# Final residual stage of a two-layer sandwich block: pairs of tiles against single tiles in a two-buffer ring

## The chip, the cores and the metric

The kernel runs on the eight NeuronCores of one Trainium2 chip. Each core computes 2,048 of the 16,384 tokens; the cores exchange nothing. The metric is the device time of the slowest core in microseconds.

## The reference

All of it is in float32; the kernel computes the matmuls in bf16.

```python
# x: [4, 4096, 4096]; W_attn, W_base: [4096, 4096]; 8 experts of rank 16, top 2
x = x + layernorm(layernorm(x) @ W_attn.T + b_attn)
y = layernorm(x)
w = top-2 softmax weights of y @ W_router.T, renormalised
lora = einsum('ter,eor,te->to', einsum('td,erd->ter', y, lora_A), lora_B, w) * 2.0
x = x + layernorm(y @ W_base.T + b_base + lora)
```

## The kernel before, in words

Everything is stored transposed: the feature index lies on the 128 partitions, the tokens along the free dimension. A core takes its tokens in four chunks (`ch`) of `C` = 512, and within a chunk the 4,096 features are 32 tiles (`k`) of 128 x 512. `xt` holds the chunk's x in float32 (32 tiles), `u` the normalised input of a matmul in bf16, `zb` the output of a matmul in bf16.

The instructions of the five engines are written out in order by hand, with semaphores: `s_t`, `s_v`, `s_s`, `s_gc` count finished instructions of TensorE, VectorE (DVE), ScalarE (ACT) and GpSimd (POOL); `s_x` counts x loads (one for each group of 8 tiles), `s_w` weight loads, and `s_o[0]`, `s_o[1]` output stores from the buffers `ost0` and `ost1`. Each engine works through its list in order, and a wait holds whatever stands behind it on that engine.

A chunk runs through these stages:

1. x load and statistics (L217 to L252). ScalarE issues the load of a group of 8 tiles (L227), after waiting at L221 until POOL has done the final add of the eighth tile of that group in the previous chunk (`f6k[8 * g + 7]`), since that add still reads `xt`. Then it makes a bf16 copy (L233) and a square (L234) of each of the 8 tiles, and TensorE sums both over the features. The load of the next group stands behind these on ScalarE.
2. The row statistics (`ln_rows`, `bc_pair`), and DVE's normalised `u` (L269 to L276).
3. 32 weight tiles of 128 x 4224 and their matmuls into `P` (L344), evacuated by ScalarE into `zb` (L328). POOL's queue issues the weight loads (L290, L301); in the first chunk the weights come in float32 and SP's queue stores them back in bf16 (`wsc`) for the other chunks.
4. Statistics, and the first residual add into `xt` (L370 to L379), in pairs of tiles.
5. Statistics of the new x, `u` again (L426 to L433), the router, and the low-rank part.
6. The second matmul with 32 weight tiles (L538), evacuated in the same way.
7. Statistics, and the final residual stage (L559 to L583): for each tile, DVE subtracts the mean from `zb` into `yb[k % 2]` and multiplies by the inverse deviation in place, POOL adds `xt` and writes `ost[k % 2]` in float32 (L574), and SP's queue stores it to `out` (L578), 256 KB.

Stage 7 is the one that the diff touches. DVE takes its tiles in pairs: two subtractions (L565, L567), one wait for the second of them, two multiplies (L570, L571), and before every pair but the first the waits of L562 to L564 for the stores of both buffers and for the add of the previous odd tile. POOL adds the two tiles one after the other, and each store is issued after its own add. On POOL's list the next chunk's first two weight loads stand behind the last add of stage 7. ScalarE's stage 1 of the next chunk runs beside stage 7 of this one, as far as the wait of L221 lets it.

Of the kernel before, what the change touches and what calls it, by code (L numbers as in the profile page):

```python
# [14 lines left out]
C = 512  # L15
NCH = TOK // C
KT = D // 128
# [6 lines left out]
def build_nc():  # L24
# [10 lines left out]
    outd = nc.dram_tensor("out", [D, TOK], F32, kind="ExternalOutput").ap()  # L35
# [3 lines left out]
    cnt = {"t": 0, "v": 0, "s": 0, "g": 0, "gc": 0,  # L39
           "x": [0, 0, 0, 0], "w": [0, 0], "o": [0, 0], "wsc": [0, 0]}  # L40

    def emit(e, fn):
        ops[e].append(fn)

    def wait(e, sem, val):
        if val > 0:
            emit(e, lambda eng, sem=sem, val=val: eng.wait_ge(sem, val))

    with ExitStack() as _es:
        xt = _es.enter_context(nc.sbuf_tensor("xt", [128, KT * C], F32))  # L50
        u = _es.enter_context(nc.sbuf_tensor("u", [128, KT * C], BF16))
        zb = _es.enter_context(nc.sbuf_tensor("zb", [128, OC * C], BF16))
# [16 lines left out]
        mbc_bf = _es.enter_context(nc.sbuf_tensor("mbc_bf", [128, C], BF16))  # L69
        ibc_bf = _es.enter_context(nc.sbuf_tensor("ibc_bf", [128, C], BF16))  # L70
# [36 lines left out]
        s_v = _es.enter_context(nc.semaphore("s_v"))  # L107
# [12 lines left out]
        s_gc = _es.enter_context(nc.semaphore("s_gc"))  # L120
# [4 lines left out]
        ost = [ost0, ost1]  # L125
# [3 lines left out]
        s_o = [s_o0, s_o1]  # L129
# [10 lines left out]
        def v_inc(fn):  # L140
            cnt["v"] += 1
            emit("V", lambda v, fn=fn: fn(v).then_inc(s_v, 1))
            return cnt["v"]

        def s_inc(fn):
            cnt["s"] += 1
            emit("S", lambda s, fn=fn: fn(s).then_inc(s_s, 1))
            return cnt["s"]

        def g_inc(fn):  # L150
            cnt["gc"] += 1
            emit("G", lambda g, fn=fn: fn(g).then_inc(s_gc, 1))
            return cnt["gc"]
# [25 lines left out]
        nout = 0  # L179
# [33 lines left out]
        f6k = {}  # L213
        for ch in range(NCH):
            t_pair = {}
            s_pair = {}
            for k in range(KT):  # L217
                if k % 8 == 0:
                    g = k // 8
# [45 lines left out]
            yb = [ybf0, ybf1]  # L265
            for kp in range(0, KT, 2):
                if kp >= 2:
# [3 lines left out]
                r2 = v_inc(lambda v, kp=kp: v.tensor_sub(  # L271
                    yb[1][:], xt[:, (kp + 1) * C:(kp + 2) * C], mbc_bf[:]))
# [94 lines left out]
            for kp in range(0, KT, 2):  # L367
                if kp >= 2:
# [3 lines left out]
                r2 = v_inc(lambda v, kp=kp: v.tensor_sub(  # L372
                    yb[1][:], zb[:, (kp + 1) * C:(kp + 2) * C], mbc_bf[:]))
                wait("V", s_v, r2)
                vc0 = v_inc(lambda v: v.tensor_mul(yb[0][:], yb[0][:], ibc_bf[:]))  # L375
                vc1 = v_inc(lambda v: v.tensor_mul(yb[1][:], yb[1][:], ibc_bf[:]))
# [30 lines left out]
            r = v_inc(lambda v: v.tensor_scalar_mul(row_a[:], ps_sqq[0:1, :], 1.0 / D))  # L407
            wait("V", s_v, r)
            r = v_inc(lambda v: v.tensor_mul(row_b[:], row_m[:], row_m[:]))
            wait("V", s_v, r)  # L410
            r = v_inc(lambda v: v.tensor_sub(row_a[:], row_a[:], row_b[:]))
# [4 lines left out]
            r = s_inc(lambda s: s.activation(row_b[:], row_a[:], AF.Ln))  # L416
# [6 lines left out]
            for kp in range(0, KT, 2):  # L423
                if kp >= 2:
# [3 lines left out]
                r2 = v_inc(lambda v, kp=kp: v.tensor_sub(  # L428
                    yb[1][:], xt[:, (kp + 1) * C:(kp + 2) * C], mbc_bf[:]))
# [29 lines left out]
            for tt in range(4):  # L459
# [17 lines left out]
                r2 = v_inc(lambda v, tt=tt: v.reduce_max(m2s[:, tt:tt + 1], l2t[:],  # L477
                                                         axis=AX.X))
# [78 lines left out]
            vv_stats_read = va  # L557
            bc_f = bc_pair(row_zm, va, sa, vv_apply_bank_free, s_free_need=vv_u_done)
            wait("V", s_s, bc_f)  # L559
            for kp in range(0, KT, 2):  # L560
                if kp >= 2:
                    wait("V", s_o[0], cnt["o"][0])  # L562
                    wait("V", s_o[1], cnt["o"][1])
                    wait("V", s_gc, f6k[kp - 1])  # L564
                v_inc(lambda v, kp=kp: v.tensor_sub(yb[0][:],  # L565
                                                    zb[:, kp * C:(kp + 1) * C], mbc_bf[:]))
                r2 = v_inc(lambda v, kp=kp: v.tensor_sub(  # L567
                    yb[1][:], zb[:, (kp + 1) * C:(kp + 2) * C], mbc_bf[:]))
                wait("V", s_v, r2)
                vc0 = v_inc(lambda v: v.tensor_mul(yb[0][:], yb[0][:], ibc_bf[:]))  # L570
                vc1 = v_inc(lambda v: v.tensor_mul(yb[1][:], yb[1][:], ibc_bf[:]))  # L571
                for k, vc in ((kp, vc0), (kp + 1, vc1)):
                    wait("G", s_v, vc)
                    f6k[k] = g_inc(lambda g, k=k: g.tensor_add(  # L574
                        ost[k % 2][:], yb[k % 2][:], xt[:, k * C:(k + 1) * C]))
                    wait("Y", s_gc, f6k[k])
                    def ostore(y, ch=ch, k=k):
                        return y.dma_start(  # L578
                            outd[k * 128:(k + 1) * 128, ch * C:(ch + 1) * C],
                            ost[k % 2][:]).then_inc(s_o[k % 2], 16)  # L580
                    emit("Y", ostore)
                    nout += 1
                    cnt["o"][k % 2] += 16  # L583
            vv_f6_done = cnt["v"]
            sv_zb_free = cnt["v"]
            vv_apply_bank_free = cnt["v"]
# [84 lines left out]
```

## Time and profile before

| | us |
|---|---|
| median of the runs | 3528.05 (3523.74 to 3532.36, 2 runs) |
| time of the profiled execution | 3537.88 |
| its span, slowest core (core 1) | 3536.3 |
| its spans, all cores | 3508.0 to 3536.3 |

| engine or transfer | busy us or share | count |
|---|---|---|
| TensorE matmul | 2381.8 (67%) | 10204 |
| DVE | 531.3 (15%) | 1243 |
| ScalarE | 544.5 (15%) | 1001 |
| POOL | 434.2 (12%) | 521 |
| x loads, `xt<-xT` | 10.3 us from issue to landing, 2048 KB each | 16 |
| output stores, `out<-ost` | 2.1 us from issue to landing, 256 KB each | 128 |

Busy shares are averages over stages with different limits, so they don't say what bounds a stage. The chain that ended last is followed back from the last instruction, at each step to what released it; "issue" in it is time in which the engine waited for nothing that the profile shows, and where an instruction begins before its forerunner has ended, only the part up to that start is counted. DVE is VectorE, POOL is GpSimd, ACT is ScalarE, ACTq and SPq are the queues that issue transfers. Times are microseconds from the span's start.

### The profile page before, as it was taken

To read this page: it belongs to the slowest core of one execution; us is meant where nothing else is said; L and a number is where in the kernel's file an instruction comes from. 1 tells how busy PE (TensorE), PEld (TensorE's weight loads), DVE (VectorE), ACT (ScalarE), POOL (GpSimd) and SP (SyncE) were. 2 spreads that over 40 slices of the span, in tenths; PEclk is the share of its full clock that TensorE was granted. 3 is DMA by queue.
4 is the path that set the end of the run, shared out by engine and by line. 5 is a ranking of instruction groups with operands and counts; after the bars stand their busy time and mean duration, and the time that the engine had idled before them with its cause. 6 is when DMAs were issued, how large, how long until landed. Compare 5 with 4: busy or idle time off the path is not lost.

```text
span 3536.3 us, 27097 instructions; the slowest of 8 cores (3508.0 to 3536.3 us)
## 1 busy us (share of the span) xinstructions
PE 2381.8 (67%) x10204; PEld 970.3 (27%) x10204; DVE 531.3 (15%) x1243; ACT 544.5 (15%) x1001; POOL 434.2 (12%) x521
## 2 busy tenths in 40 slices
PE   2677744787713998289922899359952699539980
PEld 0233311333200443034400344024420244114430
DVE  0400025000024000510012300340011400250002
ACT  3001021010121111211113011201102111211110
POOL 0000031000030001300021000400013000310003
PEclk7689965998855999589965799579975799659995
DMA  6399912888641442023333243013334143003422
GB/s 169 79 201 204 201 51 49 196 200 196 145 147 66 135 143 90 25 86 135 136 112 114 86 147 136 25 37 135 135 111 165 49 147 137 35 25 136 143 95 89
DMA packets 81887, 417.09 MB, mean 118 GB/s; under 512 B 7648, under 2 KB 7776, under 8 KB 40544
## 3 DMA queue, kind: packets, MB, share of 16 engines
q0 software_dynamic: 37472, 279.04, 29.6%
q1 hardware_dynamic: 27648, 102.77, 7.4%
q10 hardware_dynamic: 16640, 33.56, 2.9%
q8 instruction: 83, 1.36, 0.2%
q14 instruction: 44, 0.36, 0.0%
HBM read 383.98 MB, written 102.76 MB: 138 GB/s over the span
## 4 chain that ended last, share of the span: by engine, by line
PE 48%; DMA 22%; DVE 14%; issue 7%; POOL 5%; ACT 3%; DVEq 0%; POOLq 0%; ACTq 0%; SPq 0%
PE P L538 21%; PE P L344 20%; DMA wb<-wA 5%; DMA wb<-wF 5%; DMA out<-ost 4%; DMA wsc<-wb 4%; DMA xt<-xT 3%; POOL xt L379 3%; POOL ost L574 3%; PE ps_sq L310 1%; DVE ybf L269 1%; DVE ybf L426 1%; DMA wb<-wsc 1%; DVE ybf L428 1%; DVE ybf L271 1%
## 5 line engine op out<-in xcount | busy, mean ns | idle before, releaser
L344 PE MATMUL P<-u,wb 128*128 128x512 bf16 x4096 | 970.4, 395 | 161.2 <-DVE u L274 90.2
L538 PE MATMUL P<-u,wb 128*128 128x512 bf16 x4096 | 936.9, 388 | 77.4 <-DMA wb<-wF 66.8
L344 PEld LDWEIGHTS P<-u,wb 128*128 128x128 bf16 x4096 | 404.1, 100 | 720.8 <-issue 285.5
L538 PEld LDWEIGHTS P<-u,wb 128*128 128x128 bf16 x4096 | 403.9, 100 | 597.0 <-issue 147.2
L328 ACT CAST zb<-P 128x512 bf16<-128x512 f32 x256 | 150.0, 586 | 2030.1 <-PE P L349 835.1
L184 DVE TENSOR_SCALAR row_zm<-ps_sq 1x512 f32<-1x512 f32 x8 | 5.4, 679 | 2174.9 <-PE ps_sqq L316 2174.9
L242 PE MATMUL ps_sq<-xbf,ones 128*1 128x512 bf16 x128 | 56.8, 540 | 390.3 <-ACT sq L234 390.3
L301 POOL DMA_DIRECT2D wb<-wsc x192 | 101.5, 529 | 1701.6 <-PE P L546 846.5
L574 POOL TENSOR_TENSOR ost<-ybf,xt 128x512 f32<-128x512 bf16 x128 | 148.4, 1178 | 381.7 <-DVE ybf L570 367.2
L379 POOL TENSOR_TENSOR xt<-xt,ybf 128x512 f32<-128x512 f32 x128 | 147.8, 1173 | 212.7 <-DVE ybf L375 207.3
L396 PE MATMUL ps_sqq<-sq,ones 128*1 128x512 bf16 x64 | 37.4, 585 | 195.7 <-ACT sq L389 195.7
L329 ACT ACTIVATE sq<-P 128x512 bf16<-128x512 f32 x256 | 154.2, 602 | 0.0
L242 PEld LDWEIGHTS ps_sq<-xbf,ones 128*1 128x1 bf16 x128 | 7.3, 80 | 439.7 <-issue 439.7
L233 ACT CAST xbf<-xt 128x512 bf16<-128x512 f32 x128 | 77.5, 606 | 319.7 <-DMA xt<-xT 319.3
L443 PE MATMUL ps_mix<-rTs,u 128*128 128x8 bf16 x512 | 31.5, 167 | 130.5 <-DVE u L431 119.6
L389 ACT ACTIVATE sq<-xt 128x512 bf16<-128x512 f32 x128 | 80.6, 630 | 170.3 <-POOL xt L379 170.3
L234 ACT ACTIVATE sq<-xt 128x512 bf16<-128x512 f32 x128 | 79.9, 624 | 0.0
L565 DVE TENSOR_TENSOR ybf<-zb,mbc_bf 128x512 bf16<-128x512 bf16 x64 | 27.2, 425 | 328.0 <-DMA out<-ost 301.4
L396 PEld LDWEIGHTS ps_sqq<-sq,ones 128*1 128x1 bf16 x64 | 5.1, 79 | 255.7 <-issue 255.7
L310 PE MATMUL ps_sq<-zb,ones 128*1 128x512 bf16 x256 | 65.5, 378 | 11.0 <-ACT sq L329 11.0
L290 POOL DMA_DIRECT2D wb<-wA x32 | 16.9, 531 | 427.1 <-PE P L349 311.8
L443 PEld LDWEIGHTS ps_mix<-rTs,u 128*128 128x128 bf16 x512 | 23.7, 104 | 144.3 <-issue 144.3
(96 smaller groups left out, 1186.9 us busy)
## 6 DMA issues: line engine op xcount, KB each, us to landing
wb<-wsc POOLq DMA_DIRECT2D x192, 1056.0 KB, 5.9
wsc<-wb SPq DMA_DIRECT2D x64, 1056.0 KB, 8.4
wb<-wA POOLq DMA_DIRECT2D x32, 1056.0 KB, 11.7
wb<-wF POOLq DMA_DIRECT2D x32, 1056.0 KB, 11.2
xt<-xT ACTq DMA_DIRECT2D x16, 2048.0 KB, 10.3
out<-ost SPq DMA_DIRECT2D x128, 256.0 KB, 2.1
aTs<-aT POOLq DMA_DIRECT2D x1, 1024.0 KB, 14.2
bTs<-bT POOLq DMA_DIRECT2D x1, 1024.0 KB, 20.7
```

Of the source, the lines that this page charges most:

```text
L233: s_inc(lambda s, k=k: s.copy(xbf[k % 4][:], xt[:, k * C:(k + 1) * C]))
L234: s_pair[k] = s_inc(lambda s, k=k: s.activation(sq[k % 4][:], xt[:, k * C:(k + 1) * C], AF.Square))
L242: t_run(lambda t, j=j: t.matmul(ps_sq[0:1, :], ones128[:, 0:1], xbf[j % 4][:], start=(j == 0), stop=(j == KT - 1)))
L301: emit("G", lambda g, mat=mat, oc=oc, par=par: g.dma_start(wb[par][:], wsc[mat, oc]).then_inc(s_w[par], 16))
L310: t_run(lambda t, j=j: t.matmul(ps_sq[0:1, :], ones128[:, 0:1], zb[:, j * C:(j + 1) * C], start=(j == 0), stop=(j == OC - 1)))
L328: s_inc(lambda s, po=po: s.copy(zb[:, po * C:(po + 1) * C], P[po % 2][:]))
L329: ev[po] = s_inc(lambda s, po=po: s.activation(sq[po % 4][:], P[po % 2][:], AF.Square))
L344: t_run(lambda t, oc=oc, k=k: t.matmul(P[oc % 2][:], wb[oc % 2][:, k * 128:(k + 1) * 128], u[:, k * C:(k + 1) * C], start=(k == 0), stop=F ...
L379: c3k[k] = g_inc(lambda g, k=k: g.tensor_add(xt[:, k * C:(k + 1) * C], xt[:, k * C:(k + 1) * C], yb[k % 2][:]))
L389: s_pair[k] = s_inc(lambda s, k=k: s.activation(sq[k % 4][:], xt[:, k * C:(k + 1) * C], AF.Square))
L538: t_run(lambda t, oc=oc, k=k: t.matmul(P[oc % 2][:], wb[oc % 2][:, k * 128:(k + 1) * 128], u[:, k * C:(k + 1) * C], start=(k == 0), stop=F ...
L574: f6k[k] = g_inc(lambda g, k=k: g.tensor_add(ost[k % 2][:], yb[k % 2][:], xt[:, k * C:(k + 1) * C]))
```

## The change

Stage 7 no longer goes in pairs. Every tile has its own subtraction, its own wait and its own multiply, in the buffer `k % 2`. Before tile `k`, DVE waits for the store that last used the buffer `k % 2` (tile `k - 2`) and for the add of tile `k - 2`. Number, kind, shape and buffers of the instructions, POOL's adds and SP's stores stay as they are; the next chunk's wait on `f6k[8 * g + 7]` too. Stage 4, which has the same form of pairs, is not changed.

```diff
--- before.py
+++ after.py
@@ -557,30 +557,25 @@
             vv_stats_read = va
             bc_f = bc_pair(row_zm, va, sa, vv_apply_bank_free, s_free_need=vv_u_done)
             wait("V", s_s, bc_f)
-            for kp in range(0, KT, 2):
-                if kp >= 2:
-                    wait("V", s_o[0], cnt["o"][0])
-                    wait("V", s_o[1], cnt["o"][1])
-                    wait("V", s_gc, f6k[kp - 1])
-                v_inc(lambda v, kp=kp: v.tensor_sub(yb[0][:],
-                                                    zb[:, kp * C:(kp + 1) * C], mbc_bf[:]))
-                r2 = v_inc(lambda v, kp=kp: v.tensor_sub(
-                    yb[1][:], zb[:, (kp + 1) * C:(kp + 2) * C], mbc_bf[:]))
-                wait("V", s_v, r2)
-                vc0 = v_inc(lambda v: v.tensor_mul(yb[0][:], yb[0][:], ibc_bf[:]))
-                vc1 = v_inc(lambda v: v.tensor_mul(yb[1][:], yb[1][:], ibc_bf[:]))
-                for k, vc in ((kp, vc0), (kp + 1, vc1)):
-                    wait("G", s_v, vc)
-                    f6k[k] = g_inc(lambda g, k=k: g.tensor_add(
-                        ost[k % 2][:], yb[k % 2][:], xt[:, k * C:(k + 1) * C]))
-                    wait("Y", s_gc, f6k[k])
-                    def ostore(y, ch=ch, k=k):
-                        return y.dma_start(
-                            outd[k * 128:(k + 1) * 128, ch * C:(ch + 1) * C],
-                            ost[k % 2][:]).then_inc(s_o[k % 2], 16)
-                    emit("Y", ostore)
-                    nout += 1
-                    cnt["o"][k % 2] += 16
+            for k in range(KT):
+                if k >= 2:
+                    wait("V", s_o[k % 2], cnt["o"][k % 2])
+                    wait("V", s_gc, f6k[k - 2])
+                r = v_inc(lambda v, k=k: v.tensor_sub(yb[k % 2][:],
+                                                      zb[:, k * C:(k + 1) * C], mbc_bf[:]))
+                wait("V", s_v, r)
+                vc = v_inc(lambda v, k=k: v.tensor_mul(yb[k % 2][:], yb[k % 2][:],
+                                                       ibc_bf[:]))
+                wait("G", s_v, vc)
+                f6k[k] = g_inc(lambda g, k=k: g.tensor_add(
+                    ost[k % 2][:], yb[k % 2][:], xt[:, k * C:(k + 1) * C]))
+                wait("Y", s_gc, f6k[k])
+                def ostore(y, ch=ch, k=k):
+                    return y.dma_start(outd[k * 128:(k + 1) * 128, ch * C:(ch + 1) * C],
+                                       ost[k % 2][:]).then_inc(s_o[k % 2], 16)
+                emit("Y", ostore)
+                nout += 1
+                cnt["o"][k % 2] += 16
             vv_f6_done = cnt["v"]
             sv_zb_free = cnt["v"]
             vv_apply_bank_free = cnt["v"]
```

## Rows read from the trace of the kernel before

**Rows 1.** Page, the chain that ended last, shares of the span by line.

```profile
PE P L538 21%; PE P L344 20%; DMA wb<-wA 5%; DMA wb<-wF 5%; DMA out<-ost 4%; DMA wsc<-wb 4%; DMA xt<-xT 3%; POOL xt L379 3%; POOL ost L574 3%; PE ps_sq L310 1%; DVE ybf L269 1%; DVE ybf L426 1%; DMA wb<-wsc 1%; DVE ybf L428 1%; DVE ybf L271 1%
```

**Rows 2.** Chain of waits, shares by line, 3440 to 3530 us, then 968 to 1076 us.

```profile
by line: DMA out<-ost 34.6%; POOL ost L574 24.4%; issue 20.4%; DVE ybf L565 7.1%; DVE ybf L570 6.8%; DVE ybf L567 5.5%; DVEq L47 1.0%; SPq L47 0.3%; POOLq L47 0.3%
...
by line: DMA out<-ost 40.3%; POOL ost L574 20.8%; issue 18.8%; DMA xt<-xT 15.2%; DVE ybf L570 6.5%; DVE ybf L565 6.3%; DVE ybf L567 5.2%; DVEq L47 0.9%; ACT mbc_bf L209 0.5%; ACT ibc_bf L210 0.5%; POOLq L47 0.3%; SPq L47 0.2%; ACTq L47 0.0%
```

**Rows 3.** Chain of waits, one turn in the last chunk: start us, us, what.

```profile
3456.74 0.42 DVE ybf L565
...
3457.60 0.44 DVE ybf L570
...
3458.17 0.24 POOL ost L574
3458.41 0.93 issue
3459.34 1.16 POOL ost L574
3460.56 2.05 DMA out<-ost
...
3462.78 0.42 DVE ybf L565
```

**Rows 4.** Timeline of the same turn: start us, us, engine, line, operation.

```profile
3457.08 0.42 DVE L567 TENSOR_TENSOR ybf<-zb,mbc_bf 128x512 bf16<-128x512 bf16 x1
...
3457.94 0.42 DVE L571 TENSOR_TENSOR ybf<-ybf,ibc_bf 128x512 bf16<-128x512 bf16 x1
3458.17 2.32 POOL L574 TENSOR_TENSOR ost<-ybf,xt 128x512 f32<-128x512 bf16 x2 [3.72 <-DVE ybf L570]
```

**Rows 5.** Timeline of DVE, first and last of 16 L565 in each chunk.

```profile
968.60 0.42 DVE L565 TENSOR_TENSOR ybf<-zb,mbc_bf 128x512 bf16<-128x512 bf16 x1 [6.60 <-ACT ibc_bf L210]
...
1072.04 0.42 DVE L565 TENSOR_TENSOR ybf<-zb,mbc_bf 128x512 bf16<-128x512 bf16 x1 [4.78 <-DMA out<-ost]
...
1794.41 0.42 DVE L565 TENSOR_TENSOR ybf<-zb,mbc_bf 128x512 bf16<-128x512 bf16 x1 [6.66 <-ACT ibc_bf L210]
...
1898.52 0.42 DVE L565 TENSOR_TENSOR ybf<-zb,mbc_bf 128x512 bf16<-128x512 bf16 x1 [5.61 <-DMA out<-ost]
...
2621.04 0.42 DVE L565 TENSOR_TENSOR ybf<-zb,mbc_bf 128x512 bf16<-128x512 bf16 x1 [6.66 <-ACT ibc_bf L210]
...
2721.41 0.42 DVE L565 TENSOR_TENSOR ybf<-zb,mbc_bf 128x512 bf16<-128x512 bf16 x1 [5.34 <-DMA out<-ost]
...
3438.38 0.43 DVE L565 TENSOR_TENSOR ybf<-zb,mbc_bf 128x512 bf16<-128x512 bf16 x1 [6.66 <-ACT ibc_bf L210]
...
3529.65 0.43 DVE L565 TENSOR_TENSOR ybf<-zb,mbc_bf 128x512 bf16<-128x512 bf16 x1 [4.46 <-DMA out<-ost]
```

**Rows 6.** Chain of waits after chunk 0: stores beside a load, last load.

```profile
990.56 3.54 DMA out<-ost
...
998.09 4.65 DMA out<-ost
...
1075.87 16.45 DMA xt<-xT
```

**Rows 7.** Line L574, the first add of a pair, then both: ns min/median/max.

```profile
L574 POOL TENSOR_TENSOR ost<-ybf,xt x1: 1201/1201/1201, 3439.8 to 3439.8; 128x512 f32<-128x512 bf16 x1
...
L574 POOL TENSOR_TENSOR ost<-ybf,xt x2: 1147/1174/1201, 3439.8 to 3441.0; 128x512 f32<-128x512 bf16 x2
```

**Rows 8.** Timeline of ScalarE, x group 0 of chunk 1 and the next load.

```profile
990.56 0.43 ACTq L227 DMA_DIRECT2D xt<-xT  x1
1002.14 0.62 ACT L233 CAST xbf<-xt 128x512 bf16<-128x512 f32 x1 [33.64 <-DMA xt<-xT]
...
1010.07 0.62 ACT L234 ACTIVATE sq<-xt 128x512 bf16<-128x512 f32 x1
1018.87 0.43 ACTq L227 DMA_DIRECT2D xt<-xT  x1
```

## What the change should do to the time

> **What bounds the kernel now.** I read the page's chain first. Nearly half of it is TensorE in the two matmul loops, but the store of the finished output, `out<-ost`, and the POOL add at L574 hold 4% and 3% of the span between them [rows 1]. Those can only be on the chain in the final residual stage (L559 to L583), so I then read the chain of waits inside that stage, once in the last chunk, where nothing runs beside it, and once after chunk 0, where the next chunk's x is loaded beside it [rows 2]. In both the reader should see the same ring, DVE, POOL, store, DVE, and no TensorE at all: the stage is a latency loop, and no engine is full in it.
>
> The chain of one turn [rows 3] shows the loop's length. DVE starts the first subtraction at 3456.74 and the one of the next pair at 3462.78: 6.04 us for two tiles. The steps are: first subtraction to second 0.34; second subtraction to first multiply 0.52; first multiply to first add 0.57; first add to second add 1.17; the second add 1.16; to the store 0.06; the store's landing 2.05; landing to DVE 0.17. Sum 6.04 (the starts that the chain leaves out are in [rows 4]).
>
> **Is the whole stage on the path?** The first subtraction of the first and of the last pair of each stage [rows 5] are 15 turns apart: 103.44, 104.11, 100.37 and 91.27 us for chunks 0 to 3. The last is 15 x 6.04 = 90.6 plus 0.7. The other three have about 13, 13 and 10 us more. That is the x load: while its 2 MB are under way, the store on the chain takes 3.54 and 4.65 us and not 2.05 [rows 6]. What follows the stage waits for it: the load of the last x group starts on the last add (1075.87), lasts 16.45 us, and then come the squares, the statistics and the next matmuls. So a microsecond off the stage is a microsecond off the kernel, in each of the four chunks, unless ScalarE's own chain of x loads takes over (below).
>
> **The change, part by part.** It keeps every instruction: 32 subtractions, 32 multiplies, 32 adds and 32 stores a chunk, in the same buffers. It removes two waits: a tile no longer waits for the store and the add of the other buffer. It also gives each tile its own wait between subtraction and multiply.
>
> *The turn of one buffer.* Tile k is followed, through ost[k%2], by tile k+2. New steps: subtraction to multiply 0.52 (as second subtraction to first multiply now), multiply to add 0.57, add 1.16, to the store 0.07, landing 2.05, landing to DVE 0.17. Sum 4.54 us. What falls out of the 6.04 is the other buffer's subtraction (0.34) and its add (1.16 or so). The two buffers run side by side, so 4.54 us is again the time for two tiles, if DVE and POOL have room: POOL needs 2 x 1.16 = 2.3 of it, DVE 4 operations of 0.42, under 2.0 with their gaps. Both fit.
>
> *The added DVE wait.* A subtraction with its multiply now takes 0.52 + 0.42 us and then the next tile's subtraction queues behind it; at the start of a stage tile 1 is ready for POOL about 0.9 us after tile 0, before POOL has finished tile 0 (1.16). It hides behind that add. Without that cover it would be some 0.2 us a turn. Behind a DVE wait for a store stands only the next tile, whose own store is later. SP's queue holds only the stores here, and POOL's only the adds; the next weight loads stand behind the last add as before.
>
> *DVE and POOL at once.* Now a multiply of 0.42 us overlaps the first add by about 0.2 us (L571 at 3457.94, the add at 3458.17) [rows 4], and otherwise POOL adds alone. After the change both operations of one buffer, 0.84 us, can run during the other buffer's add. No row shows that much overlap. The overlapped first add is 1.201 us long and the pair's other 1.147 [rows 7]: 0.054 for 0.2. From below: nothing, or the 0.054 once a turn. From above, all 0.84 us is added to the add. Scaled by rows 7 it is 0.054 x 0.84/0.19 = 0.24. I take 0.06, a turn of 4.60, because the phase of the buffers is set by the add itself and part of the overlap goes to gaps.
>
> The Trainium skill, "SBUF — State Buffer", section "Who interferes with whom", is stricter: a DVE instruction with two SBUF inputs and a GpSimd instruction that reads SBUF exclude each other, and the later one waits for the whole of the earlier. By that rule the first add in rows 7 would be about 0.19 us longer than the other, where the trace has 0.054, so the trace agrees at most in part. What full exclusion would do here is the second rival below.
>
> *Beside the x loads.* A group of 8 tiles takes 4 x 6.04 + 1.49 + 2.60 = 28.25 us (the two slow landings of rows 6); the loads issued at 990.56 and 1018.87 are 28.31 apart [rows 8]. After: 4 x 4.60 = 18.4 plus the same kind of delay. A load of about 11 us meets some 1.6 turns of each buffer, each with its landing longer by 1.5 to 2.6: 2.4 to 4.2. I keep 4.1, so 22.5 us a group, and the stage keeps its 13, 13 and 10 us of extra.
>
> *What is late next.* ScalarE takes, for one group, 11.58 us from the load's issue to the first copy and 8.55 to the end of the last square: 20.13 [rows 8]. It issues the next load only then. At 28.3 us a group it now waits 8 us for the adds; at 22.5 it waits 2.4. It stays hidden, but just. This is where a larger gain would stop: the group can't get shorter than 20.1 while loads last as long.
>
> **The sum.** 15 turns x (6.04 - 4.60) = 21.6 us. The last turn ends 0.3 us earlier (the last add ends 3.41 after its even tile's first subtraction, not 3.75). 21.9 us x 4 chunks = 88 us. The profiled execution has a span of 3536.3 and a time of 3537.9, 0.3% over the median of 3528; against the median: 3528 - 88 = 3440 us, a ratio of 0.975. With no overlap cost 4 x (15 x 1.50 + 0.3) = 91, 3437; with 0.24 a turn 77, 3451.
>
> **The rivals.** About 2% (71 us, 3457) is what a measurement of this kernel can tell from no change.
> - *Exclusion.* DVE and POOL operations block each other whole. Per tile 1.09 us of DVE steps and 1.16 of add, 2.25; two tiles 4.50, which just fits in 4.54, once the blocking has pushed the buffers half a turn apart. Then no loss stays, except that each disturbance (start of a stage, each load) costs one blocked operation, up to 1.16: four a chunk, 4 x 3 + 1 = 13 times, 15 us. 3437 + 15 = 3452. For it: operations do use the same memory. Against: rows 7. This is what the skill's rule above makes of the time.
> - *The add yields and the phases do not part.* Every other add is longer by 0.84: turn 5.38, 4 x (15 x 0.66 + 0.3) = 41 us, 3487, no change that can be told. Against it again the 0.054 of rows 7.
> - *The x loads take over.* Stores now press on the loads more evenly. The last load, beside two weight loads, took 16.45 us. If every load did: 16.45 + 0.28 + 8.55 = 25.3 us a group against 28.3, 3 groups x 3.0 and the first group's 6, 15 us a chunk; 3 x 15 + 22 = 67 us, 3461. Against: stores and loads move the same bytes as before, at about 4 MB in 22.5 us.
> - *Stores slow each other (slower).* Stores from the two buffers are now under way nearly all the time. Break-even is a landing of 2.05 + 1.50 = 3.55 everywhere. At the 4.65 of rows 6 in every turn it is 7.14 a turn, 60 x 1.10 - 1 = 65 us slower, 3593. Against: now the second store starts 1.17 after the first and overlaps it for 0.9 us, and still lands in 2.05 [rows 3].
> - *Little is on the path.* Only the last chunk gains, 22 us: 3506. Against it stands the chain [rows 2, 6].
>
> **How the numbers follow.** Forecast 0.66; exclusion 0.12; yielding add 0.08; loads take over 0.07; slow stores 0.03; off the path 0.04. The time is the forecast's, 3440. The range holds the forecast with its bounds (3437 to 3451), exclusion (3452) and the loads' case (3461), together 0.85; below, the loaded landings might cost less, until ScalarE's 20.1 us a group stops it: 3 chunks x 3 groups x 2.4 = 22, 3418, of which I include most: 3421 to 3462. Faster by over 2%: forecast, exclusion and a little of the loads' case, 0.80; within 2%: 0.18; slower: 0.02.
>
> **What would show it.** In the new profile a quiet turn (first subtraction of tile k to that of k+2) of 4.5 to 4.7 us in the last chunk, its 15 turns about 69 us; adds of about 1.16 to 1.25 us; stores in the quiet stage still landing in about 2.05; x load issues 20.1 to 23 us apart; the wait of the first copy for its load 11 to 12 us. The yielding add would show as adds near 2.0 us; exclusion as gaps in front of a DVE operation that end with an add; slow stores as landings over 3.5 in the last chunk. I am wrong if the stage shrinks but the gap from its last add to the next matmuls grows, or if landings beside loads rise well over 4.7.

## The result, and the profile after

The changed kernel is faster, by less than forecast. The ratio of its time to that of the kernel before is 0.983, with a 95% interval of 0.981 to 0.986; both were timed again side by side, and 0.983 of the 3528 us that stood ahead of the forecast is 3469 us, 59 us less. Forecast were 88 us less, a ratio of 0.975, and a range of 3421 to 3462. A second comparison on the chip gave 0.981 (0.977 to 0.984). The gain is beyond the interval, but it lies under the 2% that the forecast gave a chance of 0.80 to be passed.

The profiled execution of the changed kernel has a span of 3473.3 us (core 2), against 3536.3. Its page still has the output store on the chain, where [rows 1] had it at 4%:

```profile
PE P L538 21%; PE P L344 21%; DMA out<-ost 5%; DMA wb<-wA 5%; DMA wsc<-wb 5%; DMA wb<-wF 4%; DMA xt<-xT 3%; POOL xt L379 3%; POOL ost L570 2%; PE ps_sq L310 1%; DVE ybf L269 1%; DVE ybf L426 1%; DVE ybf L428 1%; DVE ybf L271 1%; DVE ybf L564 1%
```

What answers to [rows 5] is the DVE timeline of core 2: the subtraction of tile 0 and that of tile 30 in chunks 0 to 3 (the subtraction is now L564, the multiply L567, the add L570, the store L574).

```profile
962.39 0.43 DVE L564 TENSOR_TENSOR ybf<-zb,mbc_bf 128x512 bf16<-128x512 bf16 x1 [6.66 <-ACT ibc_bf L210]
1049.72 0.43 DVE L564 TENSOR_TENSOR ybf<-zb,mbc_bf 128x512 bf16<-128x512 bf16 x1 [2.32 <-DMA out<-ost]
...
1769.79 0.42 DVE L564 TENSOR_TENSOR ybf<-zb,mbc_bf 128x512 bf16<-128x512 bf16 x1 [6.66 <-ACT ibc_bf L210]
1861.32 0.43 DVE L564 TENSOR_TENSOR ybf<-zb,mbc_bf 128x512 bf16<-128x512 bf16 x1 [2.32 <-DMA out<-ost]
...
2581.01 0.43 DVE L564 TENSOR_TENSOR ybf<-zb,mbc_bf 128x512 bf16<-128x512 bf16 x1 [6.66 <-ACT ibc_bf L210]
2667.79 0.43 DVE L564 TENSOR_TENSOR ybf<-zb,mbc_bf 128x512 bf16<-128x512 bf16 x1 [2.14 <-DMA out<-ost]
...
3387.70 0.43 DVE L564 TENSOR_TENSOR ybf<-zb,mbc_bf 128x512 bf16<-128x512 bf16 x1 [6.66 <-ACT ibc_bf L210]
3465.92 0.42 DVE L564 TENSOR_TENSOR ybf<-zb,mbc_bf 128x512 bf16<-128x512 bf16 x1 [1.56 <-DMA out<-ost]
```

Fifteen turns take 87.3, 91.5, 86.8 and 78.2 us on this core, where [rows 5] had 103.4, 104.1, 100.4 and 91.3. Forecast were 82, 82, 79 and 69.

The table takes the same measure over the cores of each profiled execution: from the first subtraction of the final stage to the end of its last add, and from there to the next chunk's first matmul (L344), with the mean landing of the stores. All are worked out from the starts and ends in the traces; "beside loads" is the mean over chunks 0 to 2 (without chunk 2 of cores 6 and 7 of the kernel before, where both run some 16 us long, which no run explains), "last" is chunk 3.

| kernel | stage beside loads, us | last stage, us | last add to next matmul, us | store landing, beside / last, us |
|---|---|---|---|---|
| before | 104.7 | 95.9 | 38.1 | 2.67 / 2.13 |
| changed | 91.7 | 77.6 | 37.8 | 3.12 / 2.31 |

So the change saves 13.0 us in each of three chunks and 18.3 in the last: 3 x 13.0 + 18.3 = 57 us, close to the 59 measured. Nothing is given back behind the stage (38.1 and 37.8). One execution fixes a stage beside loads to about 2 us only: the changed kernel profiled again, below, has 93.7 and 76.8.

### The profile page after: what moved, and what is told of

It reads as the page before. It is cut to its first block, busy times and chain, and to the rows that moved or that the text cites. A ratio compares the mean times of both kernels' runs of the same rounds, so it can differ in the third digit from the quotient of the medians.

```text
span 3473.3 us, 27221 instructions; the slowest of 8 cores (3448.5 to 3473.3 us)
## 1 busy us (share of the span) xinstructions
PE 2379.2 (69%) x10204; PEld 970.1 (28%) x10204; DVE 563.4 (16%) x1243; ACT 545.2 (16%) x1001; POOL 435.5 (13%) x521
## 4 chain that ended last, share of the span: by engine, by line
PE 49%; DMA 23%; DVE 14%; issue 5%; POOL 5%; ACT 3%; DVEq 0%; POOLq 0%; ACTq 0%; SPq 0%
PE P L538 21%; PE P L344 21%; DMA out<-ost 5%; DMA wb<-wA 5%; DMA wsc<-wb 5%; DMA wb<-wF 4%; DMA xt<-xT 3%; POOL xt L379 3%; POOL ost L570 2%; PE ps_sq L310 1%; DVE ybf L269 1%; DVE ybf L426 1%; DVE ybf L428 1%; DVE ybf L271 1%; DVE ybf L564 1%
## 5 line engine op out<-in xcount | busy, mean ns | idle before, releaser
L344 PE MATMUL P<-u,wb 128*128 128x512 bf16 x4096 | 972.6, 395 | 158.7 <-DVE u L274 90.2
L344 PEld LDWEIGHTS P<-u,wb 128*128 128x128 bf16 x4096 | 404.9, 100 | 719.3 <-issue 284.1
L570 POOL TENSOR_TENSOR ost<-ybf,xt 128x512 f32<-128x512 bf16 x128 | 149.1, 1165 | 324.4 <-DVE ybf L567 324.4
L564 DVE TENSOR_TENSOR ybf<-zb,mbc_bf 128x512 bf16<-128x512 bf16 x128 | 68.1, 532 | 239.2 <-DMA out<-ost 206.8
L567 DVE TENSOR_TENSOR ybf<-ybf,ibc_bf 128x512 bf16<-128x512 bf16 x128 | 62.1, 485 | 14.1 <-DVE ybf L564 0.9
```

The costliest lines, as they stand in the source:

```text
L344: t_run(lambda t, oc=oc, k=k: t.matmul(P[oc % 2][:], wb[oc % 2][:, k * 128:(k + 1) * 128], u[:, k * C:(k + 1) * C], start=(k == 0), stop=F ...
L564: r = v_inc(lambda v, k=k: v.tensor_sub(yb[k % 2][:], zb[:, k * C:(k + 1) * C], mbc_bf[:]))
L570: f6k[k] = g_inc(lambda g, k=k: g.tensor_add(ost[k % 2][:], yb[k % 2][:], xt[:, k * C:(k + 1) * C]))
```

## Where 21.9 us a chunk became 13: three theories

*Loads.* The stores of chunks 0 to 2 share the DMA engines with the x loads, and the new order of stores pays more for that than the old. *Exclusion.* DVE and POOL block each other. *Neighbour.* Stores are slowed by what the other cores do.

The chain of waits of the changed kernel (core 2, after chunk 0) shows the first at work; below it the timeline of ScalarE with the load's issue, the first copy behind it and the next load:

```profile
983.77 6.60 DMA out<-ost
...
992.87 2.21 DMA out<-ost
...
1007.75 6.43 DMA out<-ost
```

```profile
981.67 0.43 ACTq L227 DMA_DIRECT2D xt<-xT  x1
991.55 0.62 ACT L233 CAST xbf<-xt 128x512 bf16<-128x512 f32 x1 [29.26 <-DMA xt<-xT]
...
1005.16 0.43 ACTq L227 DMA_DIRECT2D xt<-xT  x1
```

The store issued at 983.77, 2.1 us into the load of 981.67, lands at 990.37, a microsecond before the load is in. Over all cores, the stores of the changed kernel that are issued together with a load land in 3.6 us on average (72 of them), those issued 2 or 3 us into it in 6.7 (71), those issued 6 us into it in 4.5 (62), and those after its end in 2.4. In the kernel before, no store was issued between 1 and 5 us into a load: its pairs came at 0 (3.5 us) and at 6 to 8 us (3.1 to 3.8).

The exclusion is there too. The timeline of POOL and, below it, of DVE at the start of the last stage, core 2:

```profile
3388.80 1.20 POOL L570 TENSOR_TENSOR ost<-ybf,xt 128x512 f32<-128x512 bf16 x1 [28.30 <-DVE ybf L567]
```

```profile
3389.09 1.19 DVE L567 TENSOR_TENSOR ybf<-ybf,ibc_bf 128x512 bf16<-128x512 bf16 x1
...
3394.03 1.03 DVE L564 TENSOR_TENSOR ybf<-zb,mbc_bf 128x512 bf16<-128x512 bf16 x1 [0.55 <-DMA out<-ost]
...
3399.30 1.30 DVE L564 TENSOR_TENSOR ybf<-zb,mbc_bf 128x512 bf16<-128x512 bf16 x1 [0.28 <-DMA out<-ost]
...
3456.64 0.42 DVE L564 TENSOR_TENSOR ybf<-zb,mbc_bf 128x512 bf16<-128x512 bf16 x1 [1.57 <-DMA out<-ost]
3461.28 0.43 DVE L564 TENSOR_TENSOR ybf<-zb,mbc_bf 128x512 bf16<-128x512 bf16 x1 [1.55 <-DMA out<-ost]
```

The multiply at 3389.09 begins while the add of 3388.80 runs, takes 1.19 us and not 0.42, and ends 0.3 us after that add. After three such meetings the two buffers have moved apart, and DVE is back at 0.42; the turn from 3456.64 to 3461.28 is 4.64 us. Over all cores 252 of the 2048 DVE operations of the four stages are stretched by more than 0.1 us, and each ends 0.28 us after the add that it met.

The adds are held too, when they start while a DVE operation runs. The timelines of POOL and DVE after chunk 2, core 2:

```profile
2658.15 1.31 POOL L570 TENSOR_TENSOR ost<-ybf,xt 128x512 f32<-128x512 bf16 x1 [4.60 <-DVE ybf L567]
```

```profile
2658.01 0.43 DVE L564 TENSOR_TENSOR ybf<-zb,mbc_bf 128x512 bf16<-128x512 bf16 x1
```

The add takes 1.31 us and not 1.16, and ends 1.02 us after the subtraction. Over all cores, 18 adds met a DVE operation with 0.21 to 0.43 us still to run; they took 1.22 to 1.45 us, and every one ended 1.02 us after that operation.

## Experiments

**The loads taken away.** In both kernels, the x loads of chunks 1 to 3 left out.

```diff
-                    emit("S", xload)
-                    cnt["x"][g] += 16
+                    if ch == 0:
+                        emit("S", xload)
+                        cnt["x"][g] += 16
```

> The kernel before with the x loads of chunks 1 to 3 left out (only chunk 0 loads x; the others work on what lies in xt, so the output is not the reference's). Load theory: the x loads cost the pairs about 10 us a chunk inside the final stage, since the loaded chunks took 104 us from first subtraction to last add and the last chunk 95; and the 14 to 16 us of the last group's load fall away behind it. So about 3 x (9 + 15) = 72 us less than before, a ratio near 0.98, and about 95 us for every final stage. Exclusion theory (DVE and POOL block each other) says nothing else of this kernel, since in pairs they hardly meet.

> The changed kernel with the x loads of chunks 1 to 3 left out in the same way. Load theory (a store that is issued 2 to 3 us into an x load lands only with the load's end, and that is where the gain of chunks 0 to 2 went): every final stage takes about 76 us from first subtraction to last add, 20 less than in the pair kernel without loads, so this kernel is 4 x 20 = 80 us faster than that one. Exclusion theory (the gain went into DVE and POOL operations that block each other): the stages of chunks 0 to 2 stay about 5 to 8 us above 76 even without loads, and the difference of the two kernels is near 60 us, as it is with the loads.

Ratios to before: 0.982 (0.976 to 0.988) in pairs, 0.955 (0.945 to 0.964) in single tiles. The difference, 0.0276 of some 3540 us, is 98 us (the executions compared lie 82 to 117 apart), where 80 were expected and it was 59 with the loads. The stages beside which loads had run shrink from 91.7 to 77.0 us in single tiles and from 104.7 to 99.2 in pairs; the last ones are 75.9 and 98.8. The landings in the first loadless stage of core 2 (min/median/max) are back near 2.2:

```profile
core 2 of [0, 1, 2, 3, 4, 5, 6, 7], span 3387.2 us
...
L575 SPq DMA_DIRECT2D out<-ost x32: 332/332/373, 971.1 to 1045.1; - x32
...
DMA to landing us min/median/max: 2.1/2.2/3.1
```

Without loads the change brings 22.2 us in a chunk (99.2 to 77.0), as forecast. So the loads are where the gain of chunks 0 to 2 went; the 60 us that the exclusion theory gives don't fit. That the pairs fell less than expected (99, not 95) fits the neighbours: two pairs of cores had landings of 2.3 to 2.7 us in this run's last stage.

**The exclusion taken away.** The broadcast rows are read from PSUM, so that each DVE operation has one input there.

```diff
-  zb[:, k * C:(k + 1) * C], mbc_bf[:]))
+  zb[:, k * C:(k + 1) * C], ps_mbc[:]))
-  yb[k % 2][:], yb[k % 2][:], ibc_bf[:]))
+  yb[k % 2][:], yb[k % 2][:], ps_ibc[:]))
```

> The changed kernel with the two broadcast rows of the final stage read from PSUM (ps_mbc, ps_ibc in float32) in place of their bf16 copies, so that each DVE operation there has one input in SBUF and one in PSUM. The operations take about 0.69 us in place of 0.42, as other DVE operations with a float32 operand do, so a turn is 0.53 us longer: 60 turns, 32 us more, if exclusion costs the changed kernel nothing. Exclusion theory: DVE operations of up to 1.3 us disappear, none is over 0.75, and what exclusion cost (up to 25 us if it is the whole shortfall) comes back: 7 us more than the changed kernel. Load theory: 25 to 32 us more, with the stretched DVE operations gone too.

Ratio 0.987 (0.978 to 0.996). The interval also holds the changed kernel's 0.983, so the reading goes by the traces. The DVE groups of this kernel, busy us and mean ns of one:

```profile
L564 DVE TENSOR_TENSOR ybf<-zb,ps_mbc 128x512 bf16<-128x512 bf16 x128 | 87.8, 686 | 213.5 <-DMA out<-ost 185.1 <-ACT ibc_bf L210 26.5 <-POOL ost L570 1.3
...
L567 DVE TENSOR_TENSOR ybf<-ybf,ps_ibc 128x512 bf16<-128x512 bf16 x128 | 88.1, 688 | 14.1 <-DVE ybf L564 0.9
```

Every DVE operation of the stage takes 0.69 us, none more. In the changed kernel (core 2) the two groups had means of 532 and 485 ns, against 425 for the same operation in stage 4, and single ones of 1.2 to 1.4. With 0.53 us more in each turn the stage should be 8 us longer; the last one is 83.5, 5.9 longer, the others 97.3, 5.6 longer. So taking exclusion away returns about 2 us a chunk (4 beside loads and 1 in the last, if the repeated run below is the measure). That agrees with an account of the changed kernel's turns: over 15 of them, the DVE operations are 2.6 us longer in all than 0.425 each beside loads and 1.2 in the last stage. Exclusion costs 3 x 2.6 + 1.2 = 9 us in the turns of the kernel.

The Trainium skill, "SBUF — State Buffer", section "Who interferes with whom", says that a DVE instruction with two SBUF inputs and a GpSimd instruction that reads SBUF exclude each other, and that one with a single SBUF input does not contend. Both halves agree with these traces: 1.19 us for 0.42 with two SBUF inputs, and a constant 0.69 with one input in PSUM.

**The order of the stores.** One wait put back for three tiles a chunk, so that no store is issued 2 to 3 us into a load:

```diff
                     wait("V", s_gc, f6k[k - 2])
+                if ch < NCH - 1 and k in (8, 16, 24):
+                    wait("V", s_o[1], cnt["o"][1])
```

> The changed kernel with one wait put back in three places a chunk: DVE starts tile 8, 16 and 24 only when the store of tile 7, 15, 23 has landed, so that no store is issued 2 to 3 us into an x load, as none was in the pair kernel. In the first two kernels a store issued with the load lands in 3.5 us, one issued 2 to 3 us into it in 6.65, one issued 6 us into it in 4.5: all but the first land about when the load ends. If the landing is set by the load's end, the landings over 5.5 us vanish here and nothing is gained, since the held tile's store now waits until the same moment: stages of 91 to 95 us, 0 to 12 us more than the changed kernel. If the collision itself costs (a store that arrives early in a load is treated worse), the stages shrink to about 86 us, 15 us less.

Ratio 0.988 (0.983 to 0.993). The landings in the stage after chunk 0, core 2:

```profile
core 2 of [0, 1, 2, 3, 4, 5, 6, 7], span 3475.5 us
...
L576 SPq DMA_DIRECT2D out<-ost x32: 332/332/373, 963.4 to 1055.3; - x32
...
DMA to landing us min/median/max: 2.1/2.2/4.5
```

The 6.6 us landings are gone (the longest of any core is 5.8), the mean landing beside loads falls from 3.1 to 2.75, and the stage takes 94.1 us, where it was 91.7 and, in the repeated run, 93.7. So the long landing is no loss that can be avoided by coming later: the held stores, issued 6 to 8 us into the load, still land about a microsecond after its end. Why a store issued behind a load lands with it stays open; no run tells an order of completion from a sharing of the DMA engines.

**The size of the loads.** 1 MB for 4 tiles instead of 2 MB for 8, in chunk 0 too. The slices of source and target, not shown, are halved to match.

```diff
-                if k % 8 == 0:
-                    g = k // 8
+                if k % 4 == 0:
+                    g = k // 4
...
-                        wait("S", s_gc, f6k[8 * g + 7])
+                        wait("S", s_gc, f6k[4 * g + 3])
```

> The changed kernel with x loads of 1 MB for 4 tiles, twice as many (chunk 0 too). If a store's landing is set by the load's end, the longest landings shrink with the load: a load of 1 MB should end after about 5 to 5.5 us and a store issued 2 us into it land in 3 to 4 us; there are twice as many such meetings, so the stage stays near 91 us (88 to 94). If it is the sharing of the engines by bytes alone, the same. If early stores are treated worse whatever the load's size, landings of 6 us stay and the stages grow to about 100. Behind the stage the last load is half as long and only 4 tiles are squared after it: 8 to 12 us less a chunk, so 25 to 35 us less than the changed kernel in all, a ratio of about 0.973 to before.

Ratio 0.973 (0.970 to 0.976). The load's own landings, core 2 after chunk 0:

```profile
core 2 of [0, 1, 2, 3, 4, 5, 6, 7], span 3431.8 us
...
L227 ACTq DMA_DIRECT2D xt<-xT x8: 431/431/432, 964.6 to 1045.1; - x8
...
DMA to landing us min/median/max: 6.1/6.5/14.2
```

A load of half the size takes 6.5 us against 9.7. Stores issued 3 us into one land in 4.0 (95 of them), those 6 us into one in 2.3 (81). The stage takes 90.6 us, about as before. The 32.4 us from the last add to the next matmul, against 37.8, are the gain, 5.4 a chunk rather than 8 to 12. The rest comes from chunk 0, whose loads are halved too: the first matmul starts at 96.5 us in the mean over the cores and not at 104.6 (on core 2 at 95.19 and not at 106.16). With 3 x (1.1 + 5.4) and 1.4 from the last stage that makes 29 us; the ratio lies 0.008 to 0.010 under those of the changed kernel, 27 to 35 us.

**Loads of one tile** in chunks 1 to 3, each issued by ScalarE when its own tile's add is done.

```diff
-                    if ch > 0:
-                        wait("S", s_gc, f6k[8 * g + 7])
+                    for j in range(8 * g, 8 * g + 8) if ch > 0 else ():
+                        wait("S", s_gc, f6k[j])
+                        emit("S", lambda se, ch=ch, g=g, j=j: se.dma_start(
+                            xt[:, j * C:(j + 1) * C],
+                            xT[j * 128:(j + 1) * 128, ch * C:(ch + 1) * C]).then_inc(s_x[g], 16))
+                        cnt["x"][g] += 16
...
-                    emit("S", xload)
-                    cnt["x"][g] += 16
+                    if ch == 0:
+                        emit("S", xload)
+                        cnt["x"][g] += 16
```

> The changed kernel, with the x load of chunks 1 to 3 cut into 256 KB loads of one tile, each issued by ScalarE as soon as its own tile's final add is done, where the group of 8 was loaded at once after the eighth. Load theory: no store waits behind 2 MB any more; landings stay under about 4 us, the final stages of chunks 0 to 2 shrink from 91 to about 80 us, and the last load shortens from 15 to about 4 us: 3 x (10 + 10) = 60 us less than the changed kernel, about 3420 us, ratio to before near 0.965. Exclusion theory: only the last load shortens, 30 to 35 us less, and the stages stay at 91. A third outcome, every store now meets some load and lands in 3.5 us: turns of 6.0 us, stages of 93 us.

Ratio 0.980 (0.973 to 0.987), no different from the changed kernel: the third outcome, and 5 us a stage worse than it said. Stages of 97.9 us with a mean landing of 3.61, since almost every store meets a load; the gap behind the stage shrinks from 37.8 to 28.6. The two nearly cancel: 3 x (9.2 - 6.2) = 9 us.

**The changed kernel again**, beside the kernels that follow.

> The changed kernel once more, as the reference for the runs beside it: a ratio of 0.983 to before, final stages of about 91 us in chunks 0 to 2 and 76 in the last. If the coupling of core 2 and core 3 in the first profile (landings of 2.6 us in the last chunk) was a matter of chance, all cores show 2.1 to 2.3 this time; if it belongs to those cores, they show it again.

Ratio 0.981; stages 93.7 and 76.8. The last stages of cores 2 and 3 took 75.4 and 74.2 us with landings near 2.1; this time cores 4 and 5 had 79.6 and 84.4 and landings of 2.46 and 2.70. So the long landings are not a matter of those cores, and they came in a pair of neighbours both times.

**The store taken out of the ring.** Four output buffers, and POOL in place of DVE waits for the store. The two new buffers, their semaphores and the waits on them elsewhere are not shown.

```diff
+                if k >= 4:
+                    wait("G", s_o[k % 4], cnt["o"][k % 4])
                 if k >= 2:
-                    wait("V", s_o[k % 2], cnt["o"][k % 2])
                     wait("V", s_gc, f6k[k - 2])
...
-                    ost[k % 2][:], yb[k % 2][:], xt[:, k * C:(k + 1) * C]))
+                    ost[k % 4][:], yb[k % 2][:], xt[:, k * C:(k + 1) * C]))
```

> The changed kernel with four output buffers, each with its own semaphore, in place of two; POOL, and no longer DVE, waits for the store of four tiles before. Load theory: with the store's landing out of the ring (four buffers cover about 8 us, and the long landings are 6 to 7), the stage is as long beside loads as alone and the same in all chunks: 55 to 66 us (two adds of 1.16 and DVE operations that the adds hold up). ScalarE's chain of x loads (9.8 us to land, 8.6 for the squares, 0.3) is then what bounds chunks 0 to 2: loads 19 to 20 us apart, the fourth issued about 74 us after the first subtraction, 17 earlier than now. 3 x 17 + 15 = 66 us less than the changed kernel, ratio to before about 0.964. Exclusion theory: turns of two tiles stay above 5 us and the stage at 85 us or more.

Ratio 0.950 (0.947 to 0.953), about 0.030 or 108 us less than the changed kernel beside it: more than the 66 expected, and by far the best single step. The stages take 61.7 us beside loads and 52.9 alone. The first x load is issued 14 us into the stage, where it was 19. The landings grew to a mean of 4.8 us beside loads, the longest to 12.7, more than four buffers cover, so the stage is not "as long beside loads as alone": per chunk POOL waits some 10 us for stores beside loads and nothing in the last stage. On core 2 after chunk 0, who waited for the store (us, times):

```profile
POOL ost L577: 11.7, 5
```

The sum by stages is 3 x (32.0 - 4.3) + 23.9 = 107 us against the repeated run. The last add is followed by 42.7 us to the next matmul (37.8), and the chain of waits from 990 to 1060 us (core 2) shows what bounds now:

```profile
by line: DMA xt<-xT 64.8%; ACT sq L238 17.0%; ACT xbf L237 14.3%; issue 8.9%; ACTq L47 1.0%; DVE row_m L188 1.0%; DVE row_a L190 1.0%; PE ps_sq L246 0.8%; PE ps_sqq L252 0.3%; PE ps_sqq L249 0.3%; DVEq L47 0.1%
...
1001.77 11.62 DMA xt<-xT
...
1020.06 14.13 DMA xt<-xT
...
1040.69 8.00 DMA xt<-xT
```

That is the ScalarE chain of [rows 8], load and squares in turn, with each load waiting for the squares of the last.

**Four buffers and loads of one tile; the same with PSUM rows.**

> Four output buffers and the x loads of one tile each. Load theory: in the two-buffer kernel the one-tile loads lengthened the stage (95 to 102 us, landings 3.6 us on average) and shortened the last load; with the store out of the ring only the second is left. ScalarE's work beside the stage is then 8.6 us a group without a 10 us wait in front, and the last group's load ends about 5 us after the last add: against four buffers alone some 20 to 25 us a chunk less, about 3350 us, ratio 0.945. If single loads are slow because the stores and the weight loads share the engines, the last load stays at 12 us or more and the gain is under 10 us a chunk.

> As before it, with the broadcast rows of the final stage read from PSUM, so that DVE and POOL do not hold each other up. Exclusion, as seen in the stretched DVE operations: with the stores out of the ring it is now the bound of the stage, 4.0 us for two tiles if DVE and POOL only take turns; without it DVE's four operations of 0.69 with gaps, 3.1 to 3.3 us. The final stage shrinks from about 62 to about 51 us in every chunk; in the last chunk all of that counts, in the others what ScalarE's chain leaves: 11 to 40 us less than the kernel beside it. If exclusion isn't the bound there, the longer operations make it 0 to 10 us slower.

Ratios 0.949 (0.946 to 0.952) and 0.947 (0.944 to 0.951). Both expectations missed: neither kernel gained anything beyond the interval. The stage is 60.7 us and the gap 41.1. The timeline of ScalarE in that kernel shows why:

```profile
999.36 3.06 ACTq L226 DMA_DIRECT2D xt<-xT  x5
1011.60 0.62 ACT L242 CAST xbf<-xt 128x512 bf16<-128x512 f32 x1 [12.04 <-POOL ost L582]
...
1019.65 3.45 ACTq L226 DMA_DIRECT2D xt<-xT  x5
1033.27 0.62 ACT L242 CAST xbf<-xt 128x512 bf16<-128x512 f32 x1 [13.12 <-DMA xt<-xT]
```

The loads stand behind the squares on ScalarE. While ScalarE squares, the adds run ahead, and then it issues the loads of the next group in a burst and waits 12 to 13 us, as for one load of 2 MB. The PSUM rows shorten the last stage from 52.9 to 47.5 us and the others from 60.7 to 57.2, and the gap grows by 3.4. Beside loads the two cancel, and what is left is the 5 us of the last stage. That shortening, though each DVE operation takes longer (0.69 us), shows that exclusion bounds the quiet stage once the store is out of the ring. It can be read from the four-buffer kernel too, whose multiplies average 1104 ns (core 2):

```profile
L574 DVE TENSOR_TENSOR ybf<-ybf,ibc_bf 128x512 bf16<-128x512 bf16 x128 | 141.3, 1104 | 13.7 <-DVE ybf L571 0.5
```

## Why the prediction was wrong

**The stage as a latency loop, all on the path: right.** The chain, the unchanged gap behind the stage (38.1 and 37.8) and the four-buffer kernel all show it.

**The turn of 4.54 us: right.** The quiet turn of core 2 is 4.64 with a landing of 2.15. Without loads, 15 turns take 70.9 to 73.0 us on average, 4.7 to 4.9 each, and the change brings 22 us a chunk.

**"I keep 4.1" beside the x loads: the step that failed, in its size.** The step carried the extra landing time over from the old order of stores, and counted quiet landings at 2.05. For 15 turns, the landings' excess over 2.05 us (mean over the cores, in the kernel before along the odd tiles, which carry its chain) is:

| | beside loads, us | last stage, us |
|---|---|---|
| before | 10.1 | 1.3 |
| changed | 16.3 | 4.0 |

The forecast let it stay as it was. It grew by 6.2 us in three chunks and by 2.7 in the last, 21 us in all. The prediction's own sign of being wrong, landings beside loads well over 4.7 us, came true: 6.7. About 4.3 us a load are lost in the collision itself: the buffer whose store goes with the load loses 1.5 and then 2.4, the other 4.6 and then little. With three loads that is 13 of the 16.3; the other 3 are landings of 2.2 to 2.9 clear of any load.

**Exclusion, "I take 0.06": mis-sized, from a misread row.** In the turns it costs 2.6 us a chunk beside loads and 1.2 in the last, 9 us in all, where 0.06 x 60 = 4 were allowed. The prediction took the 0.054 us of [rows 7] for a small price of 0.19 us of overlap, scaled it, and counted it against exclusion. It is exclusion at work: that add started at 3458.17 and the DVE operation ended at 3458.36 [rows 4], and 0.19 + 1.02 is its length of 1.2. An add that starts just before a DVE operation ends loses little, since its first 0.14 us (1.16 - 1.02) are not held; a DVE operation that starts during an add loses the rest of the add, and no row of before had that. It shows as a longer operation, and not as the gap in front of one that the prediction named as its sign.

**"The last turn ends 0.3 us earlier": the wrong way.** The forecast let the last add end 3.41 us after the first subtraction of tile 30. It ends 4.5 us after it (3.76 before), since the half turn between the buffers puts tile 31 about 2 us behind tile 30, where the forecast let the add of tile 31 follow that of tile 30 at once. That is 1.1 us a chunk, 4 in all. With the rows in PSUM the distance between two tiles grows from 1.4 to 1.8 us over the last stage, with exclusion from 0.9 to 2.2, so most of it is a cost of exclusion too. With it the rival's 15 us are nearly right (9 + 4), and its half turn came about as described.

Together: 88 - 21 - (9 - 4) - 4 = 58 us, against 57 to 59 measured.

**The rivals.** The x loads did not take over: their issues are 23.5 us apart in the ScalarE rows above (981.67 and 1005.16), over ScalarE's 20.1, and it still waits for the adds. The loads' case was near in time (3461) for another reason, by luck. The landing never came near the 3.55 us of break-even in a quiet stage.

## What to carry to other kernels

When a loop is bound by a transfer's landing, first count the buffers: taking two waits out brought 1.7%, two more buffers of 256 KB brought 3 points more, though even they left some 10 us a chunk of waiting on the long landings. A small store issued behind a large load landed about when the load did, so its landing was the load's remaining time and not its own price; don't carry a measured delay over to another order of issue. After the change, look at which queue the next thing stands in: cutting loads into tiles gained nothing as long as their issues stood behind ScalarE's squares.

## What the runs showed of the hardware

Stores of two neighbour cores seem to slow each other, in some executions. In the changed kernel's last stage, core 2 has landings (min/median/max) of 2.2/2.8/3.0 us while core 3 is in its stage too, and 2.1/2.1/2.2 after core 3 has ended at 3454 (each core's times count from its own first instruction, and that all start together is taken for granted here):

```profile
L574 SPq DMA_DIRECT2D out<-ost x22: 332/332/333, 3390.1 to 3445.4; - x22
...
DMA to landing us min/median/max: 2.2/2.8/3.0
...
L574 SPq DMA_DIRECT2D out<-ost x7: 332/332/333, 3456.4 to 3470.4; - x7
...
DMA to landing us min/median/max: 2.1/2.1/2.2
```

Core 3 shows the mirror image: 2.1 in the median before core 2 has begun, 2.8 from then to its end. Cores 0 and 1 overlapped just as long in the same execution and had medians of 2.1. In the repeated run it was cores 4 and 5, in the loadless pair kernel cores 2 and 3 and cores 6 and 7. The neighbour is not all of it: in the repeated run core 5 stayed at 2.4 us after core 4 had ended, above the 2.1 of other cores. That it is a matter of how the two cores' stores fall against each other in time fits this, but no run set that apart, and it stays open. The longer landings account for the 5 to 8 us by which such a stage is longer than the others.
